# Null key's products in the second loop of a two-layer decoder: one column tile of TensorE replaced by token tiles in four 32-column tiles

## The chip, the core and the metric

One core of a Trainium2 chip runs the whole program, all arithmetic in f32. The metric is the device time of one execution in microseconds (us), the median of several. TensorE is called PE below (PEld for its weight loads), VectorE DVE, ScalarE ACT, GpSimd POOL and SyncE SP.

## The reference, cut to what matters

Eight sequences of 512 tokens with 256 channels pass through two layers. Layer 0 is linear attention, cross attention and a quantized feed-forward block; layer 1 is a metric attention, a cosine cross attention with a null key, and a product in the frequency domain. Each block ends in a residual sum and a layer norm. The change lies in the cosine cross attention:

```python
def _L1_xattn_ref(x, context, g_norm, null_kv, Wq, Wkv, q_scale, k_scale, Wout, g_out):
    # 16 heads of 64 channels, SCALE = 8, 64 context rows per sequence
    q = layer_norm(x, g_norm) @ Wq
    k, v = jnp.split(context @ Wkv, 2, axis=-1)
    q, k, v = map(split_heads, (q, k, v))
    k = jnp.concatenate([nk, k], axis=2)      # nk: the null key, the same for every head
    v = jnp.concatenate([nv, v], axis=2)
    q = l2norm(q) * q_scale
    k = l2norm(k) * k_scale
    attn = jax.nn.softmax(jnp.einsum('bhid,bhjd->bhij', q, k) * SCALE, axis=-1)
    out = jnp.einsum('bhij,bhjd->bhid', attn, v)
    return layer_norm(out @ Wout, g_out)      # heads merged before Wout
```

For each token and head two numbers are needed beside the scores against the 64 context rows: the squared norm of q, and the product of q with the null key. Since q is a product of x with a weight matrix, the null key's product is x times a matrix of 16 columns that is worked out once; the kernel calls it `null_wq` (two blocks of 128 channels x 32 columns; columns 4 to 19 hold the 16 heads, the others are zero).

## The kernel before, in words

The program has two loops over the eight sequences, with the preparation of weights between them. The first loop does linear attention, cross attention and the first half of the feed-forward block, the second loop the rest. The change lies in the second loop, which the profile shows from about 700 us to the end. A sequence ("batch" b) is 512 tokens: four token tiles of 128 (`NT = 4`). Channels lie in two blocks of 128 (`NC = 2`).

The order of work is written out by hand for each engine. `unrolled` takes a list of pairs (skew, step), and in pass n it calls each step for batch n - skew; so four batches are under way in one pass: the down projection of batch n (`dn_*`), the metric attention of batch n - 1 and its end for n - 2 (`met_*`), the queries of the cosine attention for n - 2 and the rest of it with the frequency product for n - 3 (`cos_*`, `spec_*`). Engines wait for one another by semaphores. Passes 1, 2, B + 1 and B + 2 have lists of their own, with fewer steps.

On PE the end of a pass and the start of the next one run so: `spec_project` (L1467, a product for batch n - 3), `cos_norm` (L1368 and L1371), `met_scores(3)` (L1302), `cos_turn_norms` (L1378), and then, in the next pass, `cos_scores(0)` (L1393), `met_out(2)` (L1318, L1326), `dn_turn` (L1222), `met_out(3)` (L1326), `cos_scores(1)` (L1393), `met_mix` (L1337).

`cos_norm` fills one bank of PSUM, `flat(2)`, 128 partitions x 512 tokens. Its first eight products (L1368) take the squares of q, 128 rows (two heads) at a time, and sum them per head by a matrix of ones `head_sel` with 32 columns. Product j goes to partitions 32 j to 32 j + 31, that is to column tile j of the array; after both values of e each of the four column tiles holds the norms of four heads in its first four rows. Then the null key's products (L1371) are added, two products (k = 0, 1) of 32 columns by 512 tokens, both into partitions 0 to 31: rows 4 to 19 of column tile 0. Every f32 product is issued as two matmul instructions, each with its weight load, so a row "x4" of L1371 is the two products of one batch.

ACT copies the bank to SBUF (`cos_copy_norms`, L1877), PE turns it by four transposes back into the bank (`cos_turn_norms`, L1378), so that tokens lie on partitions and, for each token tile t, the 128 former rows on columns 128 t to 128 t + 127. DVE reads it in `cos_floor`: the norms with a floor (L2562), and the 16 null products of each token tile (L2564), which lie at column 128 t + 4. POOL then takes the norms to the power of -1/2, a token tile at a time (`cos_norms`, L1998, 128 x 16 each), and DVE scales the scores by them (`cos_scale`, L2577 and L2578).

On DVE `cos_floor` stands between the statistics of the frequency product (`spec_add`, L2726, L2118 to L2124) and the causal mask of the metric attention (`met_mask(3)`, L2535); then come `spec_finish` (L2130), which waits for POOL's L1938, and `cos_scale(0)`. Later in the same list `met_add` (L2543) waits for `met_mix`.

Of the kernel before, what the change touches and what calls it, by code (L numbers as in the profile page):

```python
# [23 lines left out]
P = 128  # L24
B, T, C = 8, 512, 256
NT = T // P
NC = C // P
TC = 64
LD = 32
H = 16  # L30
# [144 lines left out]
def decoder(nc, x_in, pack_ident, pack_lin, pack_ctx, pack_xat, pack_ffn, pack_l1, pack_prep,  # L175
# [4 lines left out]
    with ctx:  # L180
        def sem(name):
            return ctx.enter_context(nc.semaphore(name))
# [21 lines left out]
        def bank(k, n=1):  # L204
            return ps[:, k:k + n, :]
# [28 lines left out]
        null_wq = ar.take(NC, 32)  # L234
# [138 lines left out]
        xt4 = ar.take(NC, T)  # L373
# [4 lines left out]
        cos_nn = ar.take(NT, 2 * H)  # L378
# [28 lines left out]
        def sig(name, per=1):  # L407

            if name not in sigs:
                if name in CONTINUES:  # L410
                    before = sig(CONTINUES[name], per)
                    sigs[name] = Signal(before.sem, per, before.base + B * per)
                else:
                    sigs[name] = Signal(sem(name), per)
                if name in BY_TILES_FIRST:
                    sigs[name].base += NT - 1
                if name in BY_HALVES_LAST:
                    sigs[name].base += 1
            assert sigs[name].per == per, name
            return sigs[name]  # L420

        def wait(eng, name, b, j=None, per=1):

            s = sig(name, per)
            eng.wait_ge(s.sem, s.at(b, per if j is None else j))

        def wait_previous(eng, name, b, per=1):

            if not b.first():
                eng.wait_ge(sig(name, per).sem, sig(name, per).at(b, 0))  # L430
# [92 lines left out]
        def rows2(k, n=2):  # L523

            return bank(k, n).rearrange("p a (b c) -> p (a b) c", c=C)
# [5 lines left out]
        def flat(k, n=1):  # L531
            return bank(k, n).rearrange("p a c -> p (a c)")
# [218 lines left out]
        def _(pe):  # L751
            mm = nc.tensor.matmul
# [5 lines left out]
            for c in range(NC):  # L758
                for t in range(NT):
                    last = tr(bank(c)[:, 0, t * P:(t + 1) * P], w["ctx"][:, t, c * P:(c + 1) * P], ident)  # L760
# [4 lines left out]
            for c in range(NC):  # L765
                for k in range(NC):
                    last = mm(flat(2 + c), w["xat_wk"][:, k, c * P:(c + 1) * P],
                              ctx_t[:, k].rearrange("p a b -> p (a b)"), start=k == 0, stop=k == NC - 1)
            last.then_inc(ev("xat_k_projected"), 1)
            pe.wait_ge(ev("ctx_t2_ready"), NC)  # L770
            for b in range(B):
                for k in range(NC):
                    last = mm(rows2(4, 4)[:, b, :], ctx_t2[:, k, b].rearrange("p a b -> p (a b)"),
                              w["xat_wv"][:, k, :], start=k == 0, stop=k == NC - 1)
# [587 lines left out]
            def cos_norm(b, par):  # L1362

                wait(pe, "cos_q_squared", b, NP, NP)
                wait_previous(pe, "cos_o_copied", b, NT)
                for e in range(2):
                    for j in range(4):
                        mm(flat(2)[32 * j:32 * j + 32], w["head_sel"][:, e], cos_sq[2 * j + e],  # L1368
                           start=e == 0, stop=e == 1 and j > 0, skip_group_check=True)
                for k in range(NC):  # L1370
                    last = mm(flat(2)[0:32], null_wq[:, k], xt4[:, k],  # L1371
                              start=False, stop=k == NC - 1, skip_group_check=True)
                last.then_inc(sig("cos_q_normed").sem, 1)

            def cos_turn_norms(b, par):
# [95 lines left out]
            def keep_busy(n):  # L1471
                def step(b, par):
                    for i in range(n):
# [11 lines left out]
                (2, cos_query(4)), (1, met_scores(1)), (2, cos_query(5)), (2, cos_query(6)), (2, cos_query(7)),  # L1485
                (1, met_out(0)), (3, cos_turn_x), (1, met_out(1)), (1, met_scores(2)), (3, spec_project),
                (2, cos_norm), (1, met_scores(3)), (2, cos_turn_norms)], {
                B + 2: [(3, cos_scores(0)), (3, cos_scores(1)), (3, cos_scores(2)), (3, keep_busy(2)), (3, cos_scores(3)),
                        (3, cos_turn(0)), (3, keep_busy(1)), (3, cos_out(0)), (3, cos_turn(1)), (3, cos_out(1)), (3, cos_turn(2)),
# [7 lines left out]
                    (1, met_scores(0)), (2, cos_query(3)), (2, cos_query(4)), (1, met_scores(1)), (2, cos_query(5)),  # L1497
                    (2, cos_query(6)), (2, cos_query(7)), (1, met_out(0)), (1, met_out(1)), (1, met_scores(2)),
                    (2, cos_norm), (1, met_scores(3)), (2, cos_turn_norms)]})

        @block.scalar
# [559 lines left out]
        def _(dve):  # L2061
            v = nc.vector
# [27 lines left out]
            for c in range(NC):  # L2090
                for h in range(4):
                    last = v.tensor_scalar(kbd[:, c, :, h], kt[:, c], w["quad16"][:, h:h + 1], None, ALU.mult)
# [466 lines left out]
            def cos_floor(b, par):  # L2559
                wait(dve, "cos_n_turned", b)  # L2560
                nn = flat(2).rearrange("p (t j n) -> p t j n", t=NT, j=4)
                v.tensor_tensor(cos_nn[:, :, 0:H].rearrange("p t (j n) -> p t j n", j=4), nn[:, :, :, 0:4],  # L2562
                                cos_floor_at.unsqueeze(2).unsqueeze(3).broadcast_to([P, NT, 4, 4]), ALU.max)
                v.tensor_copy(cos_nn[:, :, H:], nn[:, :, 0, 4:4 + H]).then_inc(sig("cos_floored").sem, 1)  # L2564
                wait(dve, "cos_floored", b)

            def cos_scale(t):
# [163 lines left out]
            def spec_finish(b, par):  # L2731
                if b.last():
# [11 lines left out]
                (3, cos_o_add(1)), (3, cos_o_add(2)), (3, cos_o_stats(3)), (1, met_mask(0)), (3, cos_o_add(3)),  # L2744
                (3, cos_stats), (1, met_mask(1)), (3, cos_finish), (1, met_mask_queries(1)), (0, dn_finish),
                (1, met_mask(2)), (2, met_floor), (3, spec_add), (2, cos_floor), (1, met_mask(3)), (3, spec_finish),
                (2, cos_scale(0)), (2, cos_max(0)), (2, cos_shift(0)), (2, cos_scale(1)), (2, cos_max(1)),
                (1, met_add), (2, cos_sum(0))], {
# [3 lines left out]
                        (3, cos_o_add(0)), (3, cos_o_stats(2)), (3, cos_o_add(1)), (3, cos_o_add(2)),  # L2752
                        (3, cos_o_stats(3)), (3, cos_o_add(3)), (3, cos_stats), (3, cos_finish), (2, met_floor),
                        (3, spec_add), (2, cos_floor), (3, spec_finish), (2, cos_raw_max(0)), (2, cos_scale(0)),
                        (2, cos_scaled_max(0)), (2, cos_shift(0)), (2, cos_raw_max(1)), (2, cos_scale(1)),
                        (2, cos_scaled_max(1)), (2, cos_sum(0))],
# [10 lines left out]
                2: [(2, met_finish), (0, dn_add), (1, met_mask_queries(0)), (1, met_mask_states), (1, met_mask(0)),  # L2767
                    (1, met_mask(1)), (1, met_mask_queries(1)), (0, dn_finish), (1, met_mask(2)), (2, met_floor),
                    (2, cos_floor), (1, met_mask(3)), (2, cos_scale(0)), (2, cos_max(0)), (2, cos_shift(0)),
                    (2, cos_scale(1)), (2, cos_max(1)), (1, met_add), (2, cos_sum(0))]})  # L2770

# [79 lines left out]
```

## Time and profile before

| what | us |
|---|---|
| median of three runs | 1377.75 (1377.09 to 1378.03) |
| span of the profiled execution, first to last instruction | 1374.7 |
| PE busy | 1243.7 (90% of the span) |
| DVE busy | 1048.2 |
| ACT busy | 517.7 |
| POOL busy | 267.8 |
| L1371, the null key's products: sum of their spans on PE | 15.0 |
| L1368, the head norms | 15.4 |

The profile gives the profiled execution by its span; a total of its own beside the span is not shown. The median of the runs is 3.05 us above the span. A busy engine need not set the time: the chain of work that ended last is what does, and a group of rows can be shorter in busy time than the sum of its instructions, since matmuls overlap.

### The profile page before, as it was taken

What the parts mean: (1) busy time and instruction counts of PE and PEld (TensorE: products, weight loads), DVE (VectorE), ACT (ScalarE), POOL (GpSimd) and SP (SyncE); (2) the same over time, 40 slices, a digit from 0 to 9 for tenths busy, and PEclk for the clock granted to TensorE, in tenths of its full rate; (3) what the DMA queues carried; (4) which work ended last, traced back from release to release, by engine and by line L of the source; (5) the groups of instructions that cost most, each with busy time, mean ns of one, the idle gap of its engine ahead of it and who ended that gap; (6) DMA issues with size and microseconds to landing.
All of it is one profiled execution on the core that took longest, in us unless ns stands there. A gap on an engine that the chain in (4) does not pass through costs nothing.

```text
span 1374.7 us, 18473 instructions
## 1 busy us (share of the span) xinstructions
PE 1243.7 (90%) x7340; PEld 828.6 (60%) x7340; DVE 1048.2 (76%) x1966; ACT 517.7 (38%) x608; POOL 267.8 (19%) x194
## 2 busy tenths in 40 slices
PE   7899999997999999853779999999999999998976
PEld 4566666665644554321566776767768686766654
DVE  3578899986634789998564787969878797887777
ACT  1244334433534567587013323232322333231421
POOL 0011111112100000033100413204132141413242
PEclk9899999999999999976899999999999999999998
DMA  5001000102582045489322011100211000000000
GB/s 219 16 16 32 31 1 31 32 16 93 150 295 77 31 153 185 167 315 373 107 87 84 31 54 62 54 31 32 63 54 54 32 24 21 27 20 36 1 16 16
DMA packets 47829, 107.86 MB, mean 78 GB/s; under 512 B 10752, under 2 KB 31360, under 8 KB 44288
## 3 DMA queue, kind: packets, MB, share of 16 engines
q1 hardware_dynamic: 43584, 104.59, 21.7%
q10 hardware_dynamic: 4160, 2.10, 0.5%
q8 instruction: 59, 0.97, 0.3%
q14 instruction: 26, 0.21, 0.1%
HBM read 62.64 MB, written 44.04 MB: 78 GB/s over the span
## 4 chain that ended last, share of the span: by engine, by line
PE 74%; DVE 16%; DMA 3%; ACT 3%; issue 2%; POOL 1%; SPq 0%; POOLq 0%; ACTq 0%; DVEq 0%
PE ps L1357 8%; PE ps L1420 7%; PE ps L1236 6%; PE ps L1067 6%; PE ps L1118 4%; PE ps L817 4%; PE ps L1393 3%; PE ps L1302 3%; PE ps L965 2%; PE ps L890 2%; PE ps L1326 2%; PE ps L1337 2%; PE ps L1467 2%; DMA arena<-up_scratch 2%; PE ps L908 2%
## 5 line engine op out<-in xcount | busy, mean ns | idle before, releaser
L1420 PE MATMUL ps<-arena 128*128 128x256 f32 x512 | 120.1, 389 | 5.8 <-ACT arena L1892 5.8
L1357 PE MATMUL ps<-arena 128*128 128x512 f32 x256 | 117.6, 598 | 0.0
L1420 PEld LDWEIGHTS ps<-arena 128*128 128x128 f32 x512 | 98.6, 195 | 27.9 <-ACT arena L1892 9.9
L2535 DVE TENSOR_TENSOR arena<-ps,arena 128x2048 f32<-128x2048 f32 x32 | 73.3, 2292 | 38.1 <-PE ps L1302 37.9
L1938 POOL TENSOR_TENSOR arena<-arena 128x4 f32<-128x4 f32 x44 | 45.5, 1038 | 282.0 <-DVE arena L2124 282.0
L1998 POOL TENSOR_TENSOR arena<-arena 128x16 f32<-128x16 f32 x32 | 92.2, 2916 | 32.5 <-DVE arena L2564 32.5
L1236 PE MATMUL ps<-arena 128*128 128x256 f32 x384 | 88.2, 386 | 5.2 <-DVE arena L2456 5.2
L1067 PE MATMUL ps<-arena 128*128 128x512 f32 x192 | 83.8, 593 | 1.2 <-ACT arena L1620 1.2
L1118 PE MATMUL ps<-arena 128*128 128x512 f32 x192 | 84.4, 594 | 0.0
L1236 PEld LDWEIGHTS ps<-arena 128*128 128x128 f32 x384 | 73.0, 194 | 16.5 <-issue 7.0
L1357 PEld LDWEIGHTS ps<-arena 128*128 128x128 f32 x256 | 46.2, 190 | 48.7 <-issue 45.1
L1892 ACT ACTIVATE arena<-ps 128x1024 f32<-128x1024 f32 x32 | 32.8, 1025 | 108.0 <-PE ps L1407 108.0
L1871 ACT ACTIVATE arena<-ps 128x512 f32<-128x512 f32 x64 | 38.3, 599 | 84.7 <-PE ps L1357 84.6
L1945 POOL TENSOR_TENSOR arena<-arena 128x1024 f32<-128x1024 f32 x8 | 18.8, 2356 | 246.4 <-DVE arena L2184 246.4
L1393 PE MATMUL ps<-arena 128*128 128x128 f32 x512 | 63.1, 277 | 2.7 <-DVE arena L2578 2.7
L2130 DVE TENSOR_SCALAR arena<-arena 128x256 f32<-128x256 f32 x176 | 61.9, 418 | 3.5 <-POOL arena L1938 3.5
L1393 PEld LDWEIGHTS ps<-arena 128*128 128x128 f32 x512 | 60.2, 192 | 5.6 <-DVE arena L2578 5.0
L1118 PEld LDWEIGHTS ps<-arena 128*128 128x128 f32 x192 | 36.1, 190 | 44.1 <-issue 41.6
L1067 PEld LDWEIGHTS ps<-arena 128*128 128x128 f32 x192 | 35.9, 190 | 43.5 <-issue 41.9
L817 PE MATMUL ps<-arena 128*128 128x512 f32 x128 | 59.3, 597 | 1.3 <-ACT arena L1518 1.3
L1550 ACT ACTIVATE arena<-arena 128x1024 f32<-128x1024 f32 x32 | 33.8, 1056 | 50.6 <-DVE arena L2205 50.6
L1882 ACT ACTIVATE arena<-arena 128x1040 f32<-128x1040 f32 x32 | 34.1, 1066 | 48.8 <-POOL arena L2008 28.6
(311 smaller groups left out, 2651.9 us busy)
## 6 DMA issues: line engine op xcount, KB each, us to landing
v_scratch<-arena SPq DMA_DIRECT2D x7, 1536.0 KB, 12.9
arena<-v_scratch SPq DMA_DIRECT2D x7, 1536.0 KB, 6.8
up_scratch<-arena SPq DMA_DIRECT2D x6, 1536.0 KB, 6.0
arena<-up_scratch SPq DMA_DIRECT2D x6, 1536.0 KB, 12.6
vw_scratch<-arena SPq DMA_DIRECT2D x32, 256.0 KB, 3.8
arena<-x_scratch SPq DMA_DIRECT2D x16, 512.0 KB, 4.7
arena<-vw_scratch SPq DMA_DIRECT2D x8, 1024.0 KB
arena<-x SPq DMA_DIRECT2D x8, 512.0 KB, 5.7
```

Source lines behind the costliest of these rows:

```text
L817: last = mm(flat(t % 2), lin_xt[:, par, k, t * P:(t + 1) * P], w["lin_wkv"][:, k], start=k == 0, stop=k == NC - 1)
L1067: last = mm(flat(2 + j), wgate_t[:, k, j * P:(j + 1) * P], ffn_xt[:, par, k], start=k == 0, stop=k == NC - 1)
L1118: last = mm(flat(2 + n % 4), wup_t[:, k, j * P:(j + 1) * P], ffn_xt[:, u % 2, k], start=k == 0, stop=k == NC - 1)
L1236: last = mm(dn_rows(b, t), dn_v[:, t, j], wdown_t[:, j], start=j == 0, stop=j == NF - 1)
L1302: last = mm(flat(3 + r)[:, 256 * t:256 * t + 256], met_p[lo:hi, c, at:at + P], met_qh[lo:hi, :, at:at + P], start=True, stop=True)
L1357: last = mm(flat(p % 2), w["cos_wq"][:, k, p * P:(p + 1) * P], xt4[:, k], start=k == 0, stop=k == NC - 1)
L1393: last = mm(flat(score_bank(b, t), 2)[:, p * P:(p + 1) * P], cos_q[:, p, t * P:(t + 1) * P], cos_kb[:, par, p], start=True, stop=True)
L1420: last = mm(flat(2)[:, C:2 * C], cos_pt[:, p], cos_vw[:, par, p], start=p == 0, stop=p == NP - 1)
L1938: g.tensor_tensor(var[0], var[1], neghalf[:, 0:NT], ALU.pow)\
L1998: g.tensor_tensor(cos_nn[:, t, 0:H], cos_nn[:, t, 0:H], neghalf[:, 0:H], ALU.pow)\
L2130: last = v.tensor_scalar(y[:, t], r[:, t], mv[:, t, 0:1], rs[:, t:t + 1], ALU.subtract, ALU.mult)
L2535: v.tensor_tensor(met_s[:, n % 2].rearrange("p r t h n -> p (r t h) n"), flat(3, 4).rearrange("p (h n) -> p h n", n=P), w["causal"].unsque ...
```

## The change

The null key's product for token tile t goes to column tile t: partitions 32 t to 32 t + 31, and of the bank's 512 columns only the 128 of that token tile. So eight products of 32 columns by 128 tokens (k = 0, 1, and t = 0 to 3 inside) take the place of two of 32 columns by 512 tokens. The `stop` mark of the norms' products changes with it. After the transposes the null products of token tile t lie at column 128 t + 32 t + 4, so that DVE reads them with a step of 160 in place of 128; the copy still has 128 x 4 x 16 elements.

```diff
@@ cos_norm (PE)
                 for e in range(2):
                     for j in range(4):
                         mm(flat(2)[32 * j:32 * j + 32], w["head_sel"][:, e], cos_sq[2 * j + e],
-                           start=e == 0, stop=e == 1 and j > 0, skip_group_check=True)
+                           start=e == 0, stop=False, skip_group_check=True)
                 for k in range(NC):
-                    last = mm(flat(2)[0:32], null_wq[:, k], xt4[:, k],
-                              start=False, stop=k == NC - 1, skip_group_check=True)
+                    for t in range(NT):
+                        at = slice(t * P, (t + 1) * P)
+                        last = mm(flat(2)[32 * t:32 * t + 32, at], null_wq[:, k], xt4[:, k, at],
+                                  start=False, stop=k == NC - 1, skip_group_check=True)
                 last.then_inc(sig("cos_q_normed").sem, 1)
@@ cos_floor (DVE)
-                v.tensor_copy(cos_nn[:, :, H:], nn[:, :, 0, 4:4 + H]).then_inc(sig("cos_floored").sem, 1)
+                tiles = nn[:, 0, 0, 4:4 + H]
+                by_tile = bass.AP(tiles.tensor, tiles.offset, [tiles.ap[0], (P + 32, NT), (1, H)])
+                v.tensor_copy(cos_nn[:, :, H:], by_tile).then_inc(sig("cos_floored").sem, 1)
                 wait(dve, "cos_floored", b)
```

The rows of PE around the place, for one batch in the middle of the second loop, before the change (each row is an operation by its line, with rows x columns of its output and how often it is issued; L1302 is `met_scores`, L1326 `met_out`):

```order
L1326 MATMUL ps<-arena 32x128 x32
L1302 MATMUL ps<-arena 128x256 x8
L1368 MATMUL ps<-arena 32x512 x8
L1371 MATMUL ps<-arena 32x512 x2
L1302 MATMUL ps<-arena 128x256 x8
L1378 MATMUL ps<-arena 128x128 x4
L1393 MATMUL ps<-arena 128x128 x8
```

The same rows of the changed kernel, whose later lines are two further down:

```order
L1326 MATMUL ps<-arena 32x128 x32
L1302 MATMUL ps<-arena 128x256 x8
L1368 MATMUL ps<-arena 32x512 x8
L1373 MATMUL ps<-arena 32x128 x8
L1302 MATMUL ps<-arena 128x256 x8
L1380 MATMUL ps<-arena 128x128 x4
L1395 MATMUL ps<-arena 128x128 x8
```

Only the fourth row differs: the shape of the product and how often it is issued. Nothing changes its place on PE, and on DVE, ACT, POOL and SP the operations, their order and their waits are the same as before.

## Rows read from the trace of the kernel before

**Rows 1.** The page: shares of the chain that ended last, by engine.

```profile
PE 74%; DVE 16%; DMA 3%; ACT 3%; issue 2%; POOL 1%; SPq 0%; POOLq 0%; ACTq 0%; DVEq 0%
```

**Rows 2.** The chain that ended last, 1003 to 1036: start us, us, what.

```profile
1008.42 1.86 PE ps L1368 x16
1010.28 1.69 PE ps L1371 x4
1011.97 1.08 PE ps L1302 x16
...
1024.61 1.24 DVE arena L2543
```

**Rows 3.** The chain from 760 on: the null key's first and last batch (eight in all).

```profile
763.26 1.69 PE ps L1371 x4
...
1316.03 1.71 PE ps L1371 x4
```

**Rows 4.** Timeline around one batch: start us, us, engine line, operands, [idle before <-releaser].

```profile
1009.66 0.62 PE L1368 MATMUL ps<-arena 128*32 128x512 f32 x4
1010.09 1.88 PE L1371 MATMUL ps<-arena 128*32 128x512 f32 x4
1011.90 1.15 PE L1302 MATMUL ps<-arena 32*128 32x256 f32 x16
1013.47 1.95 PE L1393 MATMUL ps<-arena 128*128 128x128 f32 x16
```

**Rows 5.** The same stretch, the other engines.

```profile
1011.63 0.17 DVE L2124 TENSOR_SCALAR arena<-arena 128x4 f32<-128x4 f32 x1
1011.88 1.01 POOL L1938 TENSOR_TENSOR arena<-arena 128x4 f32<-128x4 f32 x1 [15.63 <-DVE arena L2124]
1012.01 0.60 ACT L1877 ACTIVATE arena<-ps 128x512 f32<-128x512 f32 x1 [8.48 <-PE ps L1371]
1013.67 0.23 DVE L2562 TENSOR_TENSOR arena<-ps,arena 128x64 f32<-128x64 f32 x1 [1.87 <-PE ps L1378]
1013.82 0.21 DVE L2564 COPY arena<-ps 128x64 f32<-128x64 f32 x1
...
1014.11 2.94 POOL L1998 TENSOR_TENSOR arena<-arena 128x16 f32<-128x16 f32 x1 [1.21 <-DVE arena L2564]
...
1017.58 0.16 DVE L2577 TENSOR_TENSOR arena<-arena 128x16 f32<-128x16 f32 x1
```

**Rows 6.** Timeline at 757 to 782: products of the new shape, and their successor.

```profile
758.37 1.95 PE L1326 MATMUL ps<-arena 128*32 128x128 f32 x64
760.26 1.15 PE L1302 MATMUL ps<-arena 32*128 32x256 f32 x16
```

**Rows 7.** Durations of single instructions of L1326 and L1302: min/median/max ns.

```profile
L1326 PE MATMUL ps<-arena x128: 272/273/297, 1000.4 to 1018.9; 128*32 128x128 f32 x128
...
L1302 PE MATMUL ps<-arena x32: 374/374/478, 1003.6 to 1012.7; 32*128 32x256 f32 x32
```

**Rows 8.** Timeline around the last batch.

```profile
1317.63 1.01 POOL L1938 TENSOR_TENSOR arena<-arena 128x4 f32<-128x4 f32 x1 [11.71 <-DVE arena L2124]
1319.53 11.73 POOL L1998 TENSOR_TENSOR arena<-arena 128x16 f32<-128x16 f32 x4 [0.89 <-DVE arena L2564]
1322.52 0.18 DVE L2577 TENSOR_TENSOR arena<-arena 128x16 f32<-128x16 f32 x1 [0.41 <-POOL arena L1998]
```

**Rows 9.** PE's timeline, 1266 to 1285: products at a low clock, then at the full one.

```profile
1269.65 1.97 PE L1407 MATMUL ps<-arena 128*128 128x128 f32 x8 [4.47 <-DVE arena L2634]
1273.12 4.67 PE L1420 MATMUL ps<-arena 128*128 128x256 f32 x16
1281.57 3.72 PE L1420 MATMUL ps<-arena 128*128 128x256 f32 x16 [1.11 <-ACT arena L1892]
```

**Rows 10.** A stretch of 1 us: length, each engine's busy us (x), granted clock of TensorE, DMA share, GB/s.

```profile
1347.00:1348.00 1.00, 1.00 (x6) 0.81 (x4) 0.92 (x5) 0.00 (x0) 0.22 (x1) 0.50 0.00 0
```

**Rows 11.** PE's timeline, 1330 to the end: the same products of L1420, twice.

```profile
1349.32 5.89 PE L1420 MATMUL ps<-arena 128*128 128x256 f32 x16 [1.11 <-ACT arena L1892]
```

## The prediction
> **What bounds the kernel now.** I read the page first. PE carries 74% of the chain of work that ended last, DVE 16% [rows 1]. That alone doesn't say that L1371 is worth anything, so the second view is the chain over one pass of the second loop [rows 2]. There the null key's products stand on the chain: L1368, L1371 and L1302 follow each other on PE without a gap, and the chain passes to DVE (L2543) only at 1024.61. L1371 takes 1.69 of it. The same piece stands on the chain in all eight batches, from 763.26 to 1316.03 [rows 3].
>
> The third view is the timeline of that place. The four instructions of L1371 (two f32 products, two instructions each) run one after the other in one column tile, from 1010.09; the sixteen of L1302 begin at 1011.90 [rows 4], 1.81 later. By contrast the last four of L1368, one in each column tile and of the same 32 columns by 512, lie within 0.62, where one alone takes 0.59 (1.88 for four of L1371, with three steps of 0.43 between them) [rows 4]. So column tiles do run side by side here, and L1371 uses one of four.
>
> **The change, step by step.** Removed are four instructions of 512 tokens in one tile; added are sixteen of 128 tokens in four tiles. What counts is the time from the first of them to the first of L1302, which stands behind them on PE.
>
> The first can start when it did before, at 1010.09: all four column tiles are done with L1368 within 0.03 of each other (0.62 less 0.59). With sixteen starts at a distance r, the last is 15 r later. The same shape, 128 rows, 32 columns, 128 tokens, cycling through four column tiles, is already in this kernel: L1326. Sixty-four of them start at 758.37 and end 1.95 later; less the 0.27 that one lasts [rows 7], the last starts at 760.05. So r = (760.05 - 758.37) / 63 = 0.027. L1302 follows there too, at 760.26: 0.21 after the last start [rows 6]. A batch therefore saves 1.81 - 0.21 - 15 r = 1.60 - 0.40 = **1.20 us**. The columns say nearly the same: a 512-token instruction takes 0.42 of the chain (1.69 / 4), a quarter of it 0.106, and four of these in each tile 0.42. With three steps of 0.106 and the 0.03 between tiles the saving would be 1.25, and no row allows more; that is the upper end.
>
> The lower end is the nearest products that do not sit in column tiles: L1393, full width, 128 tokens, sixteen in 1.95, start every 0.112 if one lasts 0.27 here too [rows 4, 7], which would save 1.60 - 1.68 = -0.08, nothing. Between them lies L1302, four row tiles of 256 tokens, with (1.15 - 0.37) / 15 = 0.052 [rows 4, 7]: it would save 0.82. I take 0.027, since L1326 is the same shape in the same kind of tile.
>
> The weight loads grow from four to sixteen a batch; L1326 pays one load per instruction too, so r holds them. The `stop` mark has no work of its own. DVE's L2564 copies the same 128 x 64 elements from the same bank, at a step of 160 for 128: I cost it at nothing: it takes 0.21 [rows 5], and nothing covers it, since it lies behind DVE's wait for the transposes; were it twice as long, it would cost 8 x 0.21 = 1.7 us in all, the bound on that side.
>
> **What moves with it, and what is late next.** ACT's copy L1877 starts when the last null product is done, and ACT had been idle for 8.48 [rows 5]; so it, the transposes L1378 and DVE's L2562 all come 1.20 earlier. DVE's own work before L2562 ends at 1011.80 and hangs on L1467, ahead of the change: of its 1.87 idle, 0.67 are left. POOL's L1998 waited 1.21 after L1938, which also hangs on that earlier work [rows 5], so it moves by all of 1.20, with 0.01 left. Were it late by a little, L2577 starts at 1017.58, 0.53 after the first L1998 has ended (1014.11 + 2.94) [rows 5]. So in the first seven batches nothing catches up, and the chain up to L2543 and beyond moves as a whole; loads and stores hang on these same engines.
>
> In the last batch POOL is idle for only 0.89 before L1998, and DVE's L2577 waits for L1998 (0.41) [rows 8]: POOL is on the chain. L1998 can come no earlier than L1938 ends (1318.64), so that batch gains 0.89.
>
> **Sum**: 7 x 1.20 + 0.89 = 9.3 us. The span of 1374.7 becomes 1365.4; the runs' median is 3.05 above the span, for work at its two ends that the change leaves alone, so the time is 1377.75 - 9.3 = **1368.5 us**.
>
> **Rivals.** (a) *The issue is the bound.* Sixteen small products with their loads could be held up by PE's queue rather than by columns. With L1302's 0.052 a batch saves 0.82, in all 6.6: 1371.2. For it speaks that there are four times as many instructions; against it L1326's 0.027. The Trainium skill, "TensorE: Matmul & The Clock Gate", section "Wait — 56ns, not 53.3ns?", speaks against the change: it says that the sequencer can spend about 62 ns on each matmul when hardware decode is off, and that this binds where a matmul's array work is shorter. By that figure a batch would save an estimated 1.60 - 0.93 = 0.67, in all 5.4, giving 1372.4. The row decides against it: 63 starts in 1.68 us [rows 6] leave no room for 62 ns each. Chance 0.05.
>
> (b) *No change.* If tiles that read different tokens of `xt4` can't stream side by side, the sixteen take as many columns in a row as the four did: r = 0.106 to 0.112, saving nothing, 1377.8. L1326's tiles all read different data (`met_s` of group g), and they do run together. Chance 0.04.
>
> (c) *Slower.* If each product waits for the one before it to finish, for its load or because it adds to a bank that other tiles are still writing, r is the whole duration, 0.27: a batch loses 15 x 0.27 - 1.60 = 2.5, eight lose 20, 1398. It decides from r above 0.107 on. For it speaks only that L1371 itself runs its instructions in turn; against it that L1368 and L1326 add into shared banks from four tiles. Chance 0.02.
>
> (d) *The clock.* In the tail L1420 is longer twice than its 3.72: 4.67 behind an idle PE of 4.47 us [rows 9], and 5.89 at 1349.32 [rows 11]; there the granted clock had fallen to 0.50 (1.2 GHz in place of 2.4) [rows 10]. L1420 alone pays 0.95 and 2.17, and the L1407 ahead of it is stretched too, so I put a fall at 2.7, an estimate. The change moves the tail by up to 9 us and takes a little work from PE, so one such stretch may be longer, shorter, gone or new: 1368.5 plus or minus 2.7, 1365.8 or 1371.2. Against it: the three runs differ by under 1 us, so the falls look steady. Chance 0.10 for both ways together.
>
> (e) *Something else comes due*, a wait between L1378 and L2543 that the rows don't show because PE hides it now, and half the gain is lost: 1373. Chance 0.03.
>
> **How the numbers follow.** The forecast, all of the gain but for tenths, has the remaining 0.76; it gives the time, 1368.5. A measurement of this kernel can tell about 0.2%, 2.8 us, from no change. All cases but (b) and (c) are faster by more than that: 0.94. (b) is the same: 0.04. (c) is slower: 0.02. For the range I take the forecast and both sides of (d), with the spread of the runs before (0.7) at the lower side and for (a), 1371.2, at the upper: 1365.5 to 1371.5. It leaves out (b), (c), (e).
>
> **What would show it.** In the changed profile the null key's row (now L1373) should show sixteen instructions in about 0.67 us a batch (15 x 0.027 + 0.27) in place of 1.88, their spans summing to some 5.4 in place of 15.0; L1302 should begin some 0.61 after the first of them in place of 1.81; the time on the chain from the first batch's null products to the last batch's should fall from 552.8 us (763.26 to 1316.03 [rows 3]) by 7 x 1.2 = 8.4; DVE's wait before L2562 should fall from 1.87 to about 0.67, and POOL's before L1998 from 1.21 to nearly nothing, in the last batch to nothing. L2564 should still take 0.21. The prediction is wrong in its central step if r is well above 0.03, wrong in "nothing catches up" if r is right and those 552.8 us shorten by less than 7.5, and wrong in the tail alone if they shorten by 8.4 and the end does not.

## The result, and the profile after

| | median us | executions | range |
|---|---|---|---|
| before | 1377.42 | 4 | 1374.71 to 1378.03 |
| changed | 1361.78 | 4 | 1359.36 to 1364.58 |

The recorded ratio is 0.9908 with a 95% interval of 0.9889 to 0.9927: faster, by 10 to 15 us (the two medians, of four executions each, lie 15.6 apart). Of the executions behind the numbers of this document two lie far off, one of the kernel before at 3272.63 us and one with two column tiles at 5142.92; they are left out of every median, range and ratio. The forecast was 1368.5 with a range of 1365.5 to 1371.5, so the direction was right and the time lies 3.7 us under the range. The profiled execution's span fell from 1374.7 to 1359.9.

First the place of the change: the timeline of the changed kernel around the batch that answers to [rows 4, 5] (start us, us, engine line, operands, idle before and what ended it; lines of DVE, ACT and POOL are higher by two or four than before). A row "x16" merges sixteen instructions.

```profile
1003.01 1.93 PE L1368 MATMUL ps<-arena 128*32 128x512 f32 x16
...
1004.75 0.62 PE L1373 MATMUL ps<-arena 128*32 128x128 f32 x16
...
1005.30 1.15 PE L1302 MATMUL ps<-arena 32*128 32x256 f32 x16
...
1006.54 1.01 POOL L1940 TENSOR_TENSOR arena<-arena 128x4 f32<-128x4 f32 x1 [15.64 <-DVE arena L2126]
...
1007.07 0.23 DVE L2564 TENSOR_TENSOR arena<-ps,arena 128x64 f32<-128x64 f32 x1 [0.61 <-PE ps L1380]
1007.21 0.21 DVE L2568 COPY arena<-ps 128x64 f32<-128x64 f32 x1
...
1007.51 8.63 POOL L2000 TENSOR_TENSOR arena<-arena 128x16 f32<-128x16 f32 x3
```

The null key's products take 0.62 in place of 1.88, and L1302 begins 0.55 after the first of them in place of 1.81. That is a gain of 1.26 a batch; the forecast had 1.20. DVE's wait before L2564 fell from 1.87 to 0.61, POOL follows L1940 without a wait, and the copy L2568, which now steps by 160, takes 0.21 as before. The spans of the null key's products sum to 5.0 us in the whole execution, 15.0 before.

The sixteen do not start evenly. In a timeline cut off at 1004.80 the row of L1373 holds the first four alone:

```profile
1004.75 0.30 PE L1373 MATMUL ps<-arena 128*32 128x128 f32 x4
```

One lasts 0.27, so these four start within 0.03 of each other. Cut at 1004.90, 1005.00 and 1005.11 the row holds eight, twelve and sixteen and takes 0.41, 0.51 and 0.62: a round of four every 0.11 us, which is a quarter of the 0.43 that one instruction of four times the columns took. So it is the columns of one tile that set the pace.

The chain of the kernel before, at the second and the sixth batch (start us, us, what):

```profile
843.74 1.86 PE ps L1368 x16
...
1173.09 1.86 PE ps L1368 x16
```

and of the changed kernel:

```profile
840.92 1.86 PE ps L1368 x16
...
1165.25 1.86 PE ps L1368 x16
```

Four passes took 329.35 us and take 324.33: 1.255 less each. So the 1.26 of the one place comes through whole in these passes.

Where the 14.8 us between the two profiled executions lie is seen when the span is cut at the first instruction of each batch's L1368, which is the last thing ahead of the change. All times are differences of such starts.

| us | before | changed | difference |
|---|---|---|---|
| start of the program to the first L1368 | 761.33 | 759.57 | -1.76 |
| first to second | 82.34 | 81.28 | -1.06 |
| second to sixth, four steps | 329.35 | 324.33 | -5.02 |
| sixth to seventh | 74.29 | 73.02 | -1.27 |
| seventh to eighth | 66.79 | 64.77 | -2.02 |
| eighth to the end of the span | 60.60 | 56.93 | -3.67 |

From the first L1368 to the eighth the time fell from 552.77 to 543.40, by 9.4 us, of which 0.8 is the longer seventh step before; the forecast had 8.4 between the same two batches.

The first row lies ahead of any changed instruction. The last two are larger than a gain of 1.26, and of 0.89, can make them. There L1420, now L1422, had been stretched while the granted clock was at half [rows 9 to 11]; in the changed kernel's execution the same operation in the last pass, which took 5.89 [rows 11], runs at its usual length:

```profile
1336.69 3.72 PE L1422 MATMUL ps<-arena 128*128 128x256 f32 x16 [1.11 <-ACT arena L1894]
```

So one profile of each says: about 9.5 us from the change, and 5 from places that compute the same as before. The experiments ask whether those 5 us belong to the change.

### The profile page after: what moved, and what is told of

It reads as the page before. It is cut to its first block, busy times and chain, and to the rows that moved or that the text cites. A ratio compares the mean times of both kernels' runs of the same rounds, so it can differ in the third digit from the quotient of the medians.

```text
span 1359.9 us, 18665 instructions
## 1 busy us (share of the span) xinstructions
PE 1228.8 (90%) x7436; PEld 823.9 (61%) x7436; DVE 1048.6 (77%) x1966; ACT 517.6 (38%) x608; POOL 271.0 (20%) x194
## 4 chain that ended last, share of the span: by engine, by line
PE 73%; DVE 18%; ACT 4%; issue 3%; DMA 2%; POOL 1%; SPq 0%; ACTq 0%; POOLq 0%; DVEq 0%
PE ps L1357 8%; PE ps L1422 7%; PE ps L1236 6%; PE ps L1067 6%; PE ps L1118 4%; PE ps L817 3%; PE ps L1302 3%; PE ps L1395 2%; PE ps L965 2%; PE ps L890 2%; PE ps L1326 2%; PE ps L1337 2%; PE ps L1469 2%; PE ps L908 2%; PE ps L1222 2%
## 5 line engine op out<-in xcount | busy, mean ns | idle before, releaser
L1422 PE MATMUL ps<-arena 128*128 128x256 f32 x512 | 116.9, 381 | 5.8 <-ACT arena L1894 5.8
L1422 PEld LDWEIGHTS ps<-arena 128*128 128x128 f32 x512 | 96.2, 190 | 26.7 <-ACT arena L1894 9.7
L1940 POOL TENSOR_TENSOR arena<-arena 128x4 f32<-128x4 f32 x44 | 45.5, 1038 | 282.0 <-DVE arena L2126 282.0
L2000 POOL TENSOR_TENSOR arena<-arena 128x16 f32<-128x16 f32 x32 | 92.4, 2920 | 23.3 <-DVE arena L2568 23.3
L1236 PE MATMUL ps<-arena 128*128 128x256 f32 x384 | 88.0, 385 | 5.3 <-DVE arena L2458 5.3
```

Of the source, the lines that this page charges most:

```text
L1236: last = mm(dn_rows(b, t), dn_v[:, t, j], wdown_t[:, j], start=j == 0, stop=j == NF - 1)
L1422: last = mm(flat(2)[:, C:2 * C], cos_pt[:, p], cos_vw[:, par, p], start=p == 0, stop=p == NP - 1)
L1940: g.tensor_tensor(var[0], var[1], neghalf[:, 0:NT], ALU.pow)\
L2000: g.tensor_tensor(cos_nn[:, t, 0:H], cos_nn[:, t, 0:H], neghalf[:, 0:H], ALU.pow)\
```

## The experiments

**Both kernels once more, unchanged**, to see how much executions of the same program differ.

> The kernel before, once more, so that each execution's granted clock is listed beside its time. Theory A (clock): the change itself is worth some 9.5 us (6 batches x 1.255 in the two chains, 1.06 in the first, 0.9 in the last); the rest of the measured difference is TensorE's granted clock in the tail, which falls or not from one execution to the next. Then executions of this kernel spread over more than 2 us, 1372 to 1379, and the longer ones have the lower mean clock. Theory B (the change speeds up the tail by itself, in every execution): this kernel stays within 1 us of 1377.5 with both falls of the clock in the tail each time.

> The changed kernel, once more. Theory A: executions spread over 1359 to 1367, the longer ones with a mean clock near 0.963, the shorter near 0.968. Theory B: within 1 us of 1361.8, the clock near 0.967 in all of them. Both: the L1368 to L1368 distance in the middle of the second loop is 81.08 us, against 82.33 before.

Measured: the kernel before 1374.42 (1370.7 to 1377.63, 12 executions), the changed one 1365.0 (1359.22 to 1366.94, 6), beside 23 further executions of the kernel before with a median of 1374.56; ratio 0.992, 0.9899 to 0.994. Both spread over some 7 us, as theory A said and B did not, and the longer executions have the lower mean clock: the six of the changed kernel stand in the same order by both, from 1359.22 us at 0.968 to 1366.94 at 0.960. The three runs known at the time of the forecast, 1377.09 to 1378.03, are from the long end of that spread. The two medians are 9.4 apart.

The steps between batches, by contrast, repeat to 0.02 us in each kernel: 82.33 to 82.35 before, 81.08 to 81.09 after (81.27 or 81.28 for the first). What differs lies ahead of the first L1368 and in the last two rows of the table. Of one and the same changed kernel, these are two profiled executions. First a group of products, L829 (start us, us, idle before), in the execution with a span of 1365.1:

```profile
37.51 3.81 PE L829 MATMUL ps<-arena 128*128 128x129 f32 x16 [1.92 <-DVE arena L2167]
```

and in one with a span of 1358.5 (from a later run):

```profile
36.99 2.05 PE L829 MATMUL ps<-arena 128*128 128x129 f32 x16 [1.93 <-DVE arena L2167]
```

The wait ahead of them is the same, and the sixteen products take nearly twice as long: the granted clock over them is 0.50 in the first execution and 1.00 in the second. The next group, L850, takes 3.89 against 2.08 after the same wait of 0.86, at the same two clocks. That is 3.6 us of stretched products, and L926 behind them starts 4.6 later (89.1 against 84.5). Then the stretch from 20 to 70 us (length, busy us and instructions of PE, PEld, DVE, ACT and POOL, granted clock, DMA share, GB/s), in the first of the two:

```profile
20.00:70.00 50.00, 41.12 (x141) 24.50 (x140) 28.35 (x60) 11.82 (x14) 3.38 (x2) 0.84 0.05 18
```

and in the second:

```profile
20.00:70.00 50.00, 40.73 (x170) 23.61 (x169) 30.81 (x62) 14.71 (x17) 3.38 (x2) 0.97 0.06 19
```

A mean granted clock of 0.84 against 0.97 from 20 to 70 us. Most of another 1.5 us come from 716 to 720, where L1326 takes 1.94 against 1.08 and L1222 1.54 against 1.07, so that the first L1368 starts 6.1 us later (764.31 against 758.19). The same code, the same places: the clock falls there in some executions for longer than in others, and the products are stretched by it, not by a wait.

**Filler in the tail.** Products that nobody reads (`keep_busy(n)`, which the kernel has already, issues n of them) are put where PE waits in the last two passes, so that PE idles less there.

```diff
+            def hold_turn(n):
+                def step(b, par):
+                    if b.off == B - 2:
+                        keep_busy(n)(b, par)
+                return step
...
-(1, met_project), (3, cos_turn(0)), (2, met_turn_x),
+(1, met_project), (3, hold_turn(4)), (3, cos_turn(0)), (2, met_turn_x),
...
-(3, cos_out(0)), (3, cos_turn(1)), (3, cos_out(1)), (3, cos_turn(2)), (3, cos_out(2)),
+(3, cos_out(0)), (3, keep_busy(1)), (3, cos_turn(1)), (3, keep_busy(1)), (3, cos_out(1)),
+(3, keep_busy(2)), (3, cos_turn(2)), (3, keep_busy(1)), (3, cos_out(2)),
```

> The kernel before with filler products on PE where it waits in the tail (four ahead of the last but one batch's first transposes, five in the last pass), so that the clock has less reason to fall there; the filler fits into waits of 4.5, 1.1, 1.3, 1.9 and 1.1 us. Theory A: the clock stays at 1.00 from 1200 us to the last output products and the time is 1372.5, 4 to 5.5 under the kernel before, where that shows both falls. Theory B: the clock is not what counts, within 1 us of the kernel before.

> The changed kernel with the same filler. Theory A: 1363 give or take 2, the clock at 1.00 in the tail, and 9.5 (8.5 to 10.5) under the kernel before with filler, since only the change itself is left between them. Theory B: 13 or more under it.

Measured: 1370.91 (1368.87 to 1376.19) and 1362.52 (1360.7 to 1363.54), 8.4 apart; in the two profiles the granted clock is 1.00 from 1250 to 1355 us, both falls gone; without filler it was 0.93 and 0.94 in the kernel before (1250 to 1300, 1300 to 1355). The later part with filler in the kernel before (columns as above):

```profile
1300.00:1355.00 55.00, 47.57 (x237) 32.57 (x237) 43.29 (x107) 14.12 (x18) 22.92 (x17) 1.00 0.03 10
```

The filler took 3.6 us from the kernel before (ratio 0.9977, 0.9964 to 0.999), a little less than the 4 to 5.5 expected, so theory B's "within 1 us" falls. The distance of the two medians, 8.4, lies just under theory A's 8.5 to 10.5 and far from B's 13; the recorded ratios, 0.9908 and 0.9977 to the same kernel before, put 9.5 us between them (0.9931). In the profiles the steps give the change's worth with no fall of the clock in either: 82.33 to 81.27 in the first, 82.34 to 81.08 four times, 74.28 to 73.02, 66.01 to 64.77, and 57.82 to 56.88 behind the last: 1.06 + 5.03 + 1.26 + 1.24 + 0.94 = 9.53 us.

**Filler ahead of the second loop too**, at the places where executions of one program differ.

```diff
+            def early_hold(n):
+                def step(b, par):
+                    if b.first():
+                        pe.wait_ge(ev("xat_v_biased"), 1)
+                        for i in range(n):
+                            mm(flat(7), ident, w["lin_wkv"][:, 0], start=True, stop=True)
...
+            def hold_first(n):
+                def step(b, par):
+                    for i in range(n):
+                        mm(flat(2), ident, w["cos_wq"][:, 0, 0:4 * P], start=True, stop=True)
...
-(2, xat_project_q), (3, xat_spread), (2, xat_scores(0)),
+(2, xat_project_q), (3, xat_spread), (2, early_hold(1)), (2, xat_scores(0)),
...
-(2, xat_scores(1)),
+(2, early_hold(3)), (2, xat_scores(1)),
...
-(1, lin_state),
+(1, early_hold(2)), (1, lin_state),
...
-1: [(1, dn_turn), (0, dn_project(0)),
+1: [(1, dn_turn), (1, hold_first(4)), (0, dn_project(0)),
...
-(1, met_out(0)), (1, met_out(1)), (1, met_scores(2)), (1, met_scores(3))],
+(1, met_out(0)), (1, hold_first(3)), (1, met_out(1)), (1, met_scores(2)), (1, hold_first(2)), (1, met_scores(3))],
```

> The kernel before with filler in the tail and also where PE waits around 37, 60 and 64 us and between 670 and 710 us, the places ahead of the change where the profiles of one and the same code differ. If the granted clock is what makes executions differ by up to 7 us, the first L1368 starts at 756 to 758 us every time (759.3 to 765.6 so far), executions lie within 3 us of each other, and the median falls under that of the kernel with filler in the tail alone (1370.9) by 2 to 4. If it is something else (transfers, the start), the spread stays 6 to 7 us.

> The changed kernel with all of that filler. With the clock as the cause of the spread: executions within 3 us of each other and 9.5 us (9 to 10) under the kernel before with the same filler, some 1358 to 1360. Otherwise: a spread of 6 us and a difference anywhere between 5 and 14.

Measured: 1365.82 (1363.64 to 1367.03, 6 executions) and 1355.45 (1354.7 to 1356.15, 4), 10.4 apart, above the 9 to 10 expected. The spread falls from 7 us to 3.4 and 1.5 (3 was expected), the first L1368 starts at 752.30 and 753.52, earlier than the 756 to 758 expected, and both kernels gain more than expected. In the stretch from 20 to 70 us the clock is now at 1.00 in both; the changed kernel's row:

```profile
20.00:70.00 50.00, 45.21 (x192) 25.10 (x191) 32.02 (x66) 14.99 (x18) 3.38 (x2) 1.00 0.05 18
```

The profile of the kernel before still has one fall in the tail, its step from the seventh to the eighth L1368 being 67.02 in place of 66.01; in the two profiles that is the 1 us by which they differ from 9.5, and whether the other executions have it too is not shown. With the stretched products above, the fall of the spread says that most of the spread is the clock's. The changed kernel with filler everywhere is the fastest version here: ratio 0.986 to the kernel before, 0.9842 to 0.9877.

**Does the rest belong to the change after all?** Two further pairs of runs, both kernels as they are.

> The changed kernel as it is, a third time, beside more runs of the kernel before on the same chip: a ratio of 0.9931 (9.5 us in 1374.5) if the change is worth what the chain says; 0.9908, as first measured, if the tail's 3.6 us belong to it.

> The kernel before as it is, once more. So far the difference of the kernels as they are is 11 to 13 us, with filler in both 8.4 and 10.4, by the chain 9.5. If the 2 us beyond 9.5 are chance (where the clock falls in the executions taken), the two kernels as they are come out 8 to 11 us apart here; if the clock falls in the tail cost the kernel before more than the changed one each time, 11 to 13 again, and this profile shows the last step from L1368 to L1368 or the rest behind it longer by 1 us or more than the fall-free 66.01 and 57.83.

> The changed kernel as it is, once more: by chance, a median of 1364 to 1366.5 beside 1374.5; if the clock costs it less in the tail, 1361.5 to 1363.5, and a profile with 64.77 for the last step and 56.91 behind it.

Measured: the third time 1362.32 beside 1374.52 (ratio 0.9905, 0.9888 to 0.9921); the fourth 1360.27 (1358.22 to 1362.51) beside 1372.79 (ratio 0.9906, 0.9886 to 0.9925), where twelve further executions of the kernel before had 1372.53. So the kernels as they are differ by 12.2 and 12.3 us here, by 9.6 in the pair above and by 15.6 in the first: more than 9.5 on the whole. The 0.9931 that the chain alone would give lies outside the interval of the third time, and "by chance" was the wrong expectation for the last pair; 1360.27 lies under the other expectation for it, 1361.5 to 1363.5, too. The profiles show part of it in the tail. What the two last rows of the table have above their fall-free values, 66.01 and 57.82 before, 64.77 and 56.88 after:

| profile | seventh to eighth L1368 | eighth to the end |
|---|---|---|
| before, the three | 0.78, 0.36, 0.00 | 2.78, 0.01, 1.66 |
| changed, the four | 0.00, 0.48, 0.00, 0.47 | 0.05, 0.03, 0.03, 0.01 |

The kernel before pays for a fall in the last pass in two of three profiles; here is the second of them, L1420 again (compare [rows 11]):

```profile
1348.28 5.31 PE L1420 MATMUL ps<-arena 128*128 128x256 f32 x16 [1.11 <-ACT arena L1892]
```

The changed kernel pays for it in none of four. Both columns together, that is 1.9 us on average against 0.3. With the change's own 9.5 this gives 11.1 of the 12 us. The first L1368, ahead of any changed instruction, also starts 2.7 us earlier on average in the four profiles than in the three (760.2 against 762.9), but single profiles of one kernel differ there by up to 6. So the shift of the tail, or the lighter work on PE, may spare the changed kernel a fall that the kernel before often has; which of the two it is, and whether seven profiles are enough to say so, stays open.

**Two column tiles in place of four**, with filler in the tail. DVE's copy of the null products (not shown) follows them to their new columns.

```diff
-                    for t in range(NT):
-                        at = slice(t * P, (t + 1) * P)
+                    for t in range(2):
+                        at = slice(2 * t * P, 2 * (t + 1) * P)
```

> The changed kernel with filler, but the null key's products in two column tiles of 256 tokens each in place of four of 128. Theory A (what counts is the columns that one tile has to take in a row): four instructions of 256 columns in each of two tiles, starts 0.213 apart, so a distance of 81.50 us from L1368 to L1368 in the middle of the second loop, 0.84 under the 82.34 of the kernel before and 0.42 over the change's 81.08. Rival (the number of instructions sets it, 0.027 each): eight instructions, 81.0 or less.

Measured: 81.50 in each of the five passes, the columns' number to the hundredth; the rival falls. (Median 1366.73, 1365.46 to 1371.28, 7 executions; ratio 0.9952, 0.9931 to 0.9974.) The eight instructions take 1.03:

```profile
1006.57 1.03 PE L1373 MATMUL ps<-arena 128*32 128x256 f32 x8
1007.54 1.15 PE L1302 MATMUL ps<-arena 32*128 32x256 f32 x16
```

**The loops exchanged**, with filler in the tail, so that a tile's four instructions follow each other.

```diff
-                for k in range(NC):
-                    for t in range(NT):
+                for t in range(NT):
+                    for k in range(NC):
```

> The changed kernel with filler, the same eight products with the loop over tiles outside and over k inside, so that the four instructions of one column tile follow each other. If PE starts products strictly in their order, a tile's first waits until the tile before has started its fourth: last start 1.3 us after the first, a distance of 82.0 us, nearly all of the gain lost. Rival (tiles take their products independently of each other): 81.08, as with the loop over tiles inside.

Measured: 81.11 to 81.13, 0.04 over the change (median 1361.13, 1359.66 to 1362.05, 4 executions; ratio 0.9908, 0.987 to 0.9946). The expectation with products started strictly in order falls by 0.9 us a pass: the sixteen take 0.66, though the first four of the program go to one tile. The row whole, and in a timeline cut off at 1004.30:

```profile
1004.22 0.66 PE L1373 MATMUL ps<-arena 128*32 128x128 f32 x16
...
1004.22 0.33 PE L1373 MATMUL ps<-arena 128*32 128x128 f32 x4
```

Four start within 0.04 of each other here too (an instruction lasts up to 0.30), and cut at 1004.40 and 1004.50 the row holds eight and twelve: again rounds of four, 0.11 apart.

**Without the null key's products**: the loop over k and t is taken out, and the semaphore is raised by the last of the norms' products.

```diff
-                        last = mm(flat(2)[32 * t:32 * t + 32, at], null_wq[:, k], xt4[:, k, at],
-                                  start=False, stop=k == NC - 1, skip_group_check=True)
```

> The changed kernel with filler, without the null key's products: the rows that they fill keep the zeros of the norms' products, so the null key's scores come out as zero. It asks how much more there was to gain and whether anything else catches up: L1371 stood on the chain for 1.69 us a batch, so 80.65 us from L1368 to L1368 if DVE and POOL follow; POOL's L1998 can come only 1.21 earlier than before, but DVE had another 0.5 in hand there. If POOL or DVE catches up, 81.0.

Measured: 80.65 or 80.66 in the middle passes after the first (median 1357.55, 2 executions), so even 1.69 a batch would come through, and 0.43 is left to the null products. DVE still waits 0.18 before the norms' floor (here L2565):

```profile
1002.46 0.22 DVE L2565 TENSOR_TENSOR arena<-ps,arena 128x64 f32<-128x64 f32 x1 [0.18 <-PE ps L1375]
```

Only the first step stays at 81.27, the same as with the change (81.28): there something else has taken over, see below.

## Why the prediction was right in its mechanism and wrong in its time

**The size of the change: right.** The forecast had 9.3 us; the steps of the pair with filler in the tail give 9.53. By its terms: 1.20 a batch came out as 1.26, because sixteen starts lie 0.35 us from first to last (0.62 less 0.27) and not 0.40. The starts come in rounds of four, as shown above, and sixteen starts have three steps between rounds; 15 times the mean distance of 63 starts counts 3.75 of them. The columns of a tile set the pace, as two tiles show too, and the upper end of 1.25 was the better value. The last batch's 0.89 came out as 0.94, with POOL going from L1940 to L2000 without a wait, as forecast (from the profile of the changed kernel):

```profile
1306.50 1.01 POOL L1940 TENSOR_TENSOR arena<-arena 128x4 f32<-128x4 f32 x1 [11.71 <-DVE arena L2126]
...
1307.47 11.72 POOL L2000 TENSOR_TENSOR arena<-arena 128x16 f32<-128x16 f32 x4
```

**"In the first seven batches nothing catches up": wrong for the first batch.** There the gain is 1.06. In that pass PE reaches L1302, `met_scores(3)`, before DVE is done with the mask that frees its banks:

```profile
759.71 2.29 DVE L2537 TENSOR_TENSOR arena<-ps,arena 128x2048 f32<-128x2048 f32 x1 [4.60 <-PE ps L1302]
...
762.05 0.74 PEld L1302 LDWEIGHTS ps<-arena 32*128 32x128 f32 x16 [0.39 <-DVE arena L2537]
```

That pass has no `spec_project` ahead of `cos_norm` to give the mask time, so PE gets there first; I had looked at a pass in the middle only. Without the null products the step is the same, 81.27, and L1302 waits for the mask again, longer:

```profile
758.73 0.74 PEld L1302 LDWEIGHTS ps<-arena 32*128 32x128 f32 x16 [1.46 <-DVE arena L2538]
```

In both profiles L1302 starts 2.48 us after the first L1368; in the kernel before it was 3.55, so 1.07 is all that this pass could gain. The mask is the bound there. It cost 0.14 us of the 1.20 that the forecast had for this batch.

**The step that failed: the sum starts from 1377.75, and rival (d) took that for steady: "the three runs differ by under 1 us, so the falls look steady".** They are not. Executions of the kernel before spread over 1369.0 to 1378.0, and 1377.75 is near the top of that. Against the 1374.5 and 1374.6 of two later medians the forecast of -9.3 would have given 1365.2; the changed kernel's medians are 1361.78, 1365.0, 1362.32 and 1360.27, so the start explains some 3 us of the miss. Three of these medians lie a further 3 to 5 us lower; the falls in the tail explain a part of that (1.6 us above), and the rest stays open. I gave (d) a chance of 0.10 and 2.7 us to either side, and counted falls in the tail alone, although the clock falls in the first 100 us and around 600 to 720 too (0.87 from 20 to 70 us, 0.70 from 600 to 640, in the profile of the kernel before), in code that the change leaves alone. The 6.7 us by which the result lies under the forecast are made up so: 5.5 between the forecast span of 1365.4 and the 1359.9 of the profile, that is 1.76 ahead of the change, 3.5 of falls that the tail did not pay this time, and 0.2 by which the change did better; and 1.2 because I put the median 3.05 above the span, as work at the two ends: every execution that is listed with its span lies 1.74 to 1.96 above it, the profiled one of the changed kernel (1361.73) 1.83, so the one before had lain near 1376.5, an estimate, under the median I started from. The range did not follow its own words either: 1365.8 less the spread of 0.7 is 1365.1, not 1365.5; the result lies under that too.

**The rivals (a), the issue, and (b), no change, fall**: the starts are 0.023 apart on average, and four of them lie within 0.03. The Trainium skill's 62 ns per matmul with hardware decode off ("TensorE: Matmul & The Clock Gate", section "Wait — 56ns, not 53.3ns?") would have made sixteen take an estimated 0.93 us from first to last start. The trace does not agree, it has 0.35, and the measurement decides. (c), slower, has nothing for it. (e), half the gain lost to another wait, has only the 0.14 us of the first batch.

## What to carry to other kernels

In a kernel like this one, products with few output columns are worth laying side by side in column tiles as soon as they stand on PE's chain, split along the moving columns if the number of results doesn't suffice; here that gave 1.26 us a batch where nothing else was due. The price of a row of the same shape elsewhere in the kernel, start to start, gave that to 0.06 us. A gain is read best as the distance between two marks inside a loop, which repeated to 0.02 us here while whole executions differed by 7. And where a profile shows the clock at half anywhere, a few runs that agree are no proof that it falls alike every time: put that cost into the range on both sides, or take the waits away with filler first, which here brought 8.7 us (1374.5 to 1365.8) by itself.

## What the runs showed of the hardware that had not been expected

One and the same program varied by 7 us within one set of runs, and by 9 over all of them, with the places and lengths of the stretches at half clock. Of the 6.6 us between two profiled executions of the changed kernel, 4.6 arose ahead of L926, mostly between 20 and 70 us, and 1.5 between 708 and 720. The same wait of 1.92 us ahead of L829 was followed by a clock of 0.50 in one execution and of 1.00 in another, so a wait alone does not tell whether the products behind it are stretched. Filler in PE's waits took the spread down to 1.5 and 3.4 us.

Column tiles do not seem to wait for each other in the order of the program: four instructions of one tile in a row, then four of the next, run as fast as with the tiles taken in turn (0.66 against 0.62 for sixteen). The Trainium skill, "TensorE: Matmul & The Clock Gate", section "The mechanism", has matmuls start and end strictly in their order; read that way sixteen would have taken an estimated 1.6 us here (1.3 between the first and the last start, and 0.27 for the last). The trace does not agree, with its rounds of four. It does not tell which instruction went to which tile, nor whether they reached PE in the order of the program, so how it comes about stays open.
